# A layer norm head moved behind the chunk loop, and weight means taken three instead of two to an eighth

## The reference, cut

```python
xn = _layernorm(x)
# branch 1: a second layer norm, a projection to 96, a convolution over 3 rows, silu,
# a selective scan with 16 states, a projection back, and xn as residual
x1 = layer_norm(xn, ln_w, ln_b) @ in_proj_W.T
...
s = y @ out_proj_W.T + xn
# branch 2: three bitlinear layers
def act_quant(x):
    scale = 127.0 / jnp.clip(jnp.max(jnp.abs(x), axis=-1, keepdims=True), EPS)
    return jnp.clip(jnp.round(x * scale), -128.0, 127.0) / scale
def weight_quant(w):
    scale = 1.0 / jnp.clip(jnp.mean(jnp.abs(w)), EPS)
    return jnp.clip(jnp.round(w * scale), -1.0, 1.0) / scale
h = _silu(bitlinear(xn, w1)) * bitlinear(xn, w3)
g = _silu(bitlinear(h, w2))
out = x + s * g
```

## Time and profile before

| | us |
|---|---|
| runs of the kernel before | 3580.67 and 3724.93, median 3652.8 |
| profiled execution | 3600.26 |
| its span on the slowest core | 3598.6 (the cores: 3579.2 to 3598.6) |
| PE busy, in the span | 2512.5 (70%) |
| DVE busy | 1863.0 (52%) |
| ACT busy | 1652.7 (46%) |
| POOL busy | 152.5 (4%) |

### The profile page before, as it was taken

The page is one execution under the profiler, slowest core; times in us unless marked ns, Lnnn a source line. Parts: engine busy times, 40 slices in busy tenths (PEclk is TensorE's granted clock), DMA queues, the critical chain, the costliest instruction groups (busy, mean ns, idle before and its releaser), DMA issues. The chain is left out here.

```text
span 3598.6 us, 29279 instructions; the slowest of 8 cores (3579.2 to 3598.6 us)
## 1 busy us (share of the span) xinstructions
PE 2512.5 (70%) x9525; PEld 1091.2 (30%) x9525; DVE 1863.0 (52%) x1805; ACT 1652.7 (46%) x1344; POOL 152.5 (4%) x283
## 2 busy tenths in 40 slices
PE   2444454996999999999999994356656734766773
PEld 1222221332444444444444442122222311322331
DVE  2545443785444544445555445445545644555564
ACT  3342432887566666666666661554443221111111
POOL 0000001111000000000000000000000000000000
PEclk9999998555999999999999997677878866888885
DMA  3021102897344444444444430554454234333213
GB/s 111 25 79 61 71 1 93 291 316 280 114 145 139 149 140 149 139 150 138 144 141 141 141 117 24 191 183 145 135 187 129 83 127 140 97 99 120 94 59 128
DMA packets 92610, 469.13 MB, mean 130 GB/s; under 512 B 12924, under 2 KB 13004, under 8 KB 58060
## 3 DMA queue, kind: packets, MB, share of 16 engines
q1 hardware_dynamic: 54412, 282.69, 23.3%
q0 software_dynamic: 38048, 184.57, 15.3%
HBM read 381.20 MB, written 85.98 MB: 130 GB/s over the span
## 5 line engine op out<-in xcount | busy, mean ns | idle before, releaser
L1513 PE MATMUL ps_f<-w2s,qhs 128*128 128x512 bf16 x2816 | 683.6, 408 | 417.7 <-DVE f_half L1532 271.9
L1072 PE MATMUL ps_a<-qx,w1q 128*128 128x512 bf16 x2816 | 629.9, 382 | 87.0 <-DVE hbuf L1117 75.1
L1080 PE MATMUL ps_b<-qx,w3q 128*128 128x512 bf16 x2816 | 622.1, 379 | 0.0
L1513 PEld LDWEIGHTS ps_f<-w2s,qhs 128*128 128x128 bf16 x2816 | 288.8, 103 | 814.3 <-issue 585.7
L1532 DVE TENSOR_TENSOR f_half<-f_half,ps_f 128x1024 f32<-128x1024 f32 x320 | 390.9, 1222 | 199.8 <-PE ps_f L1513 194.0
L1072 PEld LDWEIGHTS ps_a<-qx,w1q 128*128 128x128 bf16 x2816 | 274.4, 98 | 434.5 <-issue 116.6
L1080 PEld LDWEIGHTS ps_b<-qx,w3q 128*128 128x128 bf16 x2816 | 275.6, 98 | 332.2
L1411 ACT ACT_TABLE_LOAD x44 | 56.5, 1283 | 604.6 <-DVE fscr L1393 603.3
L1105 ACT ACT_TABLE_LOAD x88 | 112.9, 1283 | 445.7 <-DVE fscr L1096 445.7
L598 PE MATMUL ps_ip<-xnTc,inprojT_sb 128*96 128x256 f32 x256 | 145.8, 673 | 168.7 <-DVE xnTc L579 168.7
L1393 DVE TENSOR_TENSOR fscr<-hbuf,shB 128x1024 int32<-128x1024 f32 x88 | 107.8, 1225 | 264.1 <-DMA hbuf<-h_scr 231.4
(11 more groups left out here) (197 smaller groups left out, 2880.9 us busy)
## 6 DMA issues: line engine op xcount, KB each, us to landing
wstg<-w1L SPq DMA_DIRECT2D x44, 1024.0 KB, 9.2
wstg<-w3L SPq DMA_DIRECT2D x44, 1024.0 KB, 11.1
w2m<-w2T SPq DMA_DIRECT2D x88, 512.0 KB, 5.7
h_scr<-hbuf POOLq DMA_DIRECT2D x88, 512.0 KB, 4.0
hbuf<-h_scr POOLq DMA_DIRECT2D x88, 512.0 KB, 6.7
wstg<-w2T SPq DMA_DIRECT2D x30, 1024.0 KB, 9.3
wstg<-w1L POOLq DMA_DIRECT2D x22, 1024.0 KB, 7.7
wmst<-w1L POOLq DMA_DIRECT2D x22, 1024.0 KB, 9.3
```

The source lines that it names most:

```text
L1072: t.matmul(ps_a[pu][:, j * 512:(j + 1) * 512], w1q[par][:, cc * 128:(cc + 1) * 128], qx[:, cc * L + th * HALF + j * 512: cc * L + th * HAL ...
L1080: inst = t.matmul(ps_b[pu][:, j * 512:(j + 1) * 512], w3q[par][:, cc * 128:(cc + 1) * 128], qx[:, cc * L + th * HALF + j * 512: cc * L + t ...
L1513: inst = t.matmul(ps_f[pu][:, j * 512:(j + 1) * 512], qhs[sp][:, k * HALF + tt * 128: k * HALF + (tt + 1) * 128], w2s[sp][:, k * C + ch * ...
```

## The change

Two edits, both in ph01. First, emit_head_a and emit_head_b become one function, emit_head, and the callback in the chunk loop goes: the DVE part of the head of eighth e+1 is emitted behind chunk 15 of eighth e and behind emit_xdma(e+2). Second, emit_means is called with 3 instead of 2, and from e = 1 instead of e = 2. That makes 21 units in ph01 in place of 12; attn's calls are as they were, and 67 units are left for it in place of 76.

```diff
-        def emit_head_a(e):
+        def emit_head(e):
             t0 = e * TPE
...
             p4v_hist[e] = s_v.v

-        def emit_head_b(e):
-            sb1 = 3 * NTT + (e % 2) * 8
-
             @blk.tensor
...
-        def emit_chunks(e, mid_cb=None):
+        def emit_chunks(e):
...
             for cc in range(NCC):
-                if cc == 10 and mid_cb is not None:
-                    mid_cb()
...
         emit_xdma(0)
         emit_xdma(1)
-        emit_head_a(0)
-        emit_head_b(0)
+        emit_head(0)
         for e in range(NE):
             if e >= 1:
                 emit_tail(e - 1)
-            cb = (lambda e=e: emit_head_a(e + 1)) if e + 1 < NE else None
-            emit_chunks(e, cb)
+            emit_chunks(e)
             if e + 2 < NE:
                 emit_xdma(e + 2)
             if e + 1 < NE:
-                emit_head_b(e + 1)
-            if e >= 2:
-                emit_means(blk, 2, "scalar")
+                emit_head(e + 1)
+            if e >= 1:
+                emit_means(blk, 3, "scalar")
```

## The result

The changed kernel takes 3568.5 us (median of 19 runs, 3553.6 to 3724.2), the kernel before 3587.1 beside it (18 runs). The ratio is 0.9938, 95% interval 0.9916 to 0.996: 22 us less, 0.6%. A second comparison on another chip gave 0.9928 (0.9902 to 0.9953), 26 us less. The forecast was 3564 us and 36 less than the profiled execution of before. The profiled execution after takes 3553.8 us, span 3552.2; that is 46.5 less than before's. As the stages show, 34 us of it are there before the last stage begins; the rest is how these two executions happened to differ behind it.

The account below looks back on a forecast made before the run. The prediction took a chain of waits to bound the first stage, no engine being full. From the profiled 3600.3 us it took 30.5 off, added 4.2 and took 9.9 off: 3564.1 us, range 3535 to 3620.

Parts of the forecast that it names:

- The chain of waits: First stage, 60 to 564 us: no engine or DMA is full, so waits set its length of 504 us.
- Part 1, the gain: DVE's wait before the sxB copy, with the head behind the chunks: 30.5 us less, bounds 1.4 and 30.5.
- order on one queue: First-stage row copies on SP's queue wait for the 2 MB x ahead: 9.35 us against 4.50 without it.
- Part 1, the loss: Head no longer covers a PE trip among the chunks: 0.6 us more, 7 times, 4.2 us; bounds 0 and 7.
- ACT: First stage: ACT's later statistics cost nothing, about 29 us of work in a period of about 61 us.
- Part 2: End of the scan: fewer mean units there leave the last two groups empty, 9.9 us less; other bound 0.
- the nine loads: Added mean units in the first stage: their 9 MB of loads cost 0, other bound 12 us if meeting x.
- The sum: Whole kernel: 3600.3 - 30.5 + 4.2 - 9.9 = 3564.1 us, 1.0% less.
- all behind 868 us: Everything after the scan: code the change does not touch, with no change in its time entered in the sum.
- Rival B: Scan block's end does not shorten because another engine or load is late there: 3574 us, chance 0.08.
- Rival C: First stage: longer PE stops drop its clock to 0.50, adding at most 201 us, 3765 us; chance 0.03.

Follow-up runs that it names:

- the third form: Kernel before with the load of x for eighth e+2 issued behind the tail's row copies, head and mean units as before: ratio 0.9941 (0.9923 to 0.9959).
- the first expectation: Written for the head moved behind the chunks alone, mean units as in the kernel before: measured ratio to before 0.9948 (0.9917 to 0.998).

## Why the prediction was right, and where not

**The chain of waits, not a full engine, bounds the first stage.** Right: the same busy time in 24 us less on core 5 (564.2 to 540.0), 23.3 in the mean over the cores.

**Part 1, the gain.** Forecast 30.5 us, measured 66.7 - 36.3 = 30.4 on the core of the profile. This core had the longest wait of the eight; their mean is 65.7 us before and 36.3 after, so 29.4 is the gain of an average core, and that is what the third form's first stage gives (29.1). The mechanism was right in that x's landing is what the rows waited for, shown by taking x away (36.4), by moving it back (72.6), and by the first and last eighth. The prediction leaned to order on one queue as the reason, and the first expectation says so outright ("queue behind"); that was for the greater part wrong, since on another queue 20.0 of 30.4 us stayed.

**Part 1, the loss.** Forecast 4.2, measured 5.8 as the difference of two first stages. The term was mis-sized: the step took the first head's 0.62 us for the transpose behind the head, while it is 0.69 and then six times 0.80 in the others, 1.2 us more, and once DVE waited 0.60 ahead of L434 where 0.23 stood in the sum, 0.4 more.

**ACT.** Right: L408 starts without a wait, and DVE never waits for ACT's statistics.

**Part 2.** Forecast 9.9, measured 9.6: conv to m13 took 302.9 and takes 293.2. The next block starts 0.8 us behind DVE's end, where it started 0.3 behind ACT's, and the sum had left that out. Right also in its reason, since 4 units moved within attn do as much (293.0), and in that the nine loads cost nothing in the first stage (562.4 against 561.9).

**The sum.** 36 us were forecast. At the start of the last stage 34 are there: 23.3 from the first stage, 9.6 from attn, 1 to 2 from m13. In the total 22 to 27 are left. The step that failed is a silent one, that all behind 868 us, being code that the change does not touch, would take its old time. In the second comparison 5.0 of the 34.4 go as a longer last stage in the mean over the cores (1344 against 1339 in the kernel before on the same chip), and 2.5 more because the slowest core stands further above that mean. In the first comparison the cores of the kernel before are not on record, so the loss can't be split there. What lengthens the stage is open, as said.

**The forecast time and the profiled execution.** That 3564 lies so near the 3568.5 measured is in part luck: the profiled execution of before, 3600.3, lies 13 us above the median that before had in the comparison, and the smaller gain makes up for that.

**Rival B** (the block's end stays) is out by the 0.8 us between L918 and the next block. **Rival C** (PE's clock): the granted clock is 1.00 in the whole first stage after, and a chunk's wait for its transpose stays at 1.0 us, though PE now stands still for 9.6 us in the head and then, but for the small trips, through the rows. The prediction's comparison of the two levels, 0.78 against 0.85 us a matmul, came out of stretches that cut instructions off at their ends. The whole groups of eight in the kernel before take nearly the same, 6.95 us at a granted 1.00 and 6.83 at 0.53, so these matmuls don't show the level at all:

```profile
577.75 6.95 PE L788 MATMUL ps_sc<-ucv,xprojT_sb 96*6 96x512 f32 x8 [16.58 <-ACT ucv L772]
595.05 6.83 PE L788 MATMUL ps_sc<-ucv,xprojT_sb 96*16 96x512 f32 x8 [2.53 <-DVE bp_sb L798]
```

## What to carry to other kernels

In this kernel a small transfer that an engine waits for is better not started while a large one is in flight, on either of the two queues tried: moving the large one by 10 us, behind the small ones, gave more of the first stage than moving the computation did (29.1 us against 23.4). Filler work in a loop that ends in a barrier should run out before the last turn; four units less behind it were worth ten microseconds. And a gain ahead of a long stage that the change does not touch should be checked at that stage's start and again at its end, since part of it can be lost there.

## What was not expected of the hardware

DVE's wait for two row copies of 1 KB beside a 2 MB load was 8.5 to 8.7 us with the rows on POOL's queue (core 5; up to 10.7 on the later core of a pair, with mean loads on the heels of the rows) and 9.1 to 10.6 on the load's own, where it was 5.2 and 4.5 without the load. So the load costs 4.6 us or more on its own queue and still 3.2 or more on another.

Neighbouring cores that run the same program differ by 4.5 us at the end of a stage with eight loads of 2 MB, and by 9.8 with the rows on POOL's queue, where one of a pair waits longer in most eighths (68.0 us in sum on core 4, 62.0 on core 5). A kernel that reaches the last stage at the same time as before, but with neighbours 9.8 us apart, is 0.6% faster.
